# Nine k times v products per linear attention layer on GpSimd, and VectorE's own v operands only in PSUM

## The reference

```
# gated linear attention (first layer): the decay is k itself, its complement scales the key
kv[t] = decay[t] * kv[t-1] + key[t, d] * v[t, e]
h[t, e] = sum_d q[t, d] * kv[t, d, e]          ;  out = h @ out_w.T + out_b
# retention (second layer): decay is one constant per head, q scaled by 8**-0.5, then a group norm
# lightning attention (second layer): q, k, v = silu(x @ W), constant decay per head,
# then a layer norm of o and a gate: (o * sigmoid(x @ Wg1 @ Wg2)) @ Wo
```

## Time and profile before

| | |
|---|---|
| median of 3 runs | 1290.07 us (1289.89 to 1290.91) |
| the profiled execution | 1290.51 us, span 1288.8 us |
| gated loop, first scan to last z | 553.4 to 642.9 us |
| retention loop, first scan to last z | 687.0 to 774.6 us |
| lightning loop, first scan to last z | 987.3 to 1084.4 us |
| busy in the span | PE 77%, DVE 70%, ACT 39%, POOL 31% |

### The profile page before, as it was taken

How to read it: one execution, slowest core, us unless ns; L and a number is a source line. 1 busy time by engine, 2 the same in 40 slices (tenths; PEclk the granted TensorE clock), 3 DMA queues, 4 the chain that set the end, 5 groups by cost and what they waited for, 6 DMA issues and landing times. The chain is left out here.

```text
span 1288.8 us, 17437 instructions
## 1 busy us (share of the span) xinstructions
PE 989.6 (77%) x5856; PEld 498.2 (39%) x5856; DVE 903.9 (70%) x1529; ACT 507.7 (39%) x1042; POOL 400.1 (31%) x479
## 2 busy tenths in 40 slices
PE   5377898999999998686658665399966775459994
PEld 3222222222222323453543213266643444336663
DVE  6957889898888712889878995533347997643335
ACT  5234567787787685311021102033334221113333
POOL 3211111011101111444425441156633344226662
PEclk9557789899999999799679976599987985679997
DMA  6881000000000002312001211011121120101114
GB/s 127 180 188 16 2 1 1 1 2 2 2 1 2 2 2 92 118 60 65 25 1 43 72 33 33 13 38 43 43 74 59 41 63 4 33 19 42 44 42 115
DMA packets 52797, 56.18 MB, mean 44 GB/s; under 512 B 7956, under 2 KB 40092, under 8 KB 52700
## 3 DMA queue, kind: packets, MB, share of 16 engines
q1 hardware_dynamic: 47480, 44.78, 13.7%
q0 software_dynamic: 4992, 10.23, 3.0%
q10 hardware_dynamic: 240, 0.05, 0.0%
HBM read 37.94 MB, written 16.91 MB: 43 GB/s over the span
## 5 line engine op out<-in xcount | busy, mean ns | idle before, releaser
L720 DVE TENSOR_REDUCE mpart<-ps 128x2 f32<-128x1024 f32 (+3 forms) x320 | 325.2, 1060 | 63.2 <-PE ps L771 38.4
L841 ACT ACTIVATE arena<-ps 128x512 f32<-128x512 f32 (+3 forms) x640 | 292.2, 542 | 147.1 <-PE ps L788 137.8
L788 PE MATMUL ps<-arena 51*128 51x512 bf16 (+3 forms) x640 | 183.8, 375 | 14.1 <-ACT arena L841 5.7
L1071 POOL TENSOR_TENSOR arena<-arena 128x512 f32<-128x512 f32 x96 | 122.2, 1274 | 165.2 <-DVE arena L1124 165.2
L771 PE MATMUL ps<-arena 51*128 51x512 bf16 (+3 forms) x640 | 152.0, 388 | 23.5 <-DVE mpart L720 15.4
L802 PE MATMUL ps<-arena,w 128*32 128x512 f32 (+3 forms) x1280 | 161.2, 577 | 2.7 <-ACT arena L841 2.2
L690 POOL TENSOR_SCALAR_AFFINE_SELECT arena<-arena 128x512 f32<-128x512 f32 x64 | 40.6, 635 | 317.5 <-ACT arena L841 234.2
L1573 DVE COPY arena<-ps 128x128 f32<-128x128 f32 x78 | 22.7, 291 | 161.6 <-PE ps L1716 161.6
L1663 ACT ACTIVATE arena<-ps 128x512 f32<-128x512 f32 x78 | 46.6, 597 | 218.8 <-PE ps L1726 218.8
L788 PEld LDWEIGHTS ps<-arena 51*128 51x128 bf16 x640 | 50.4, 96 | 174.1 <-ACT arena L841 135.8
L1110 DVE TENSOR_TENSOR arena<-arena 128x512 f32<-128x512 f32 x62 | 102.1, 1646 | 12.4 <-ACT arena L1177 4.7
(11 more groups left out here) (263 smaller groups left out, 1490.9 us busy)
## 6 DMA issues: line engine op xcount, KB each, us to landing
w<-in_w SPq DMA_DIRECT2D x2, 2048.0 KB, 11.5
arena<-results SPq DMA_DIRECT2D x16, 256.0 KB, 4.9
arena<-g_v SPq DMA_DIRECT2D x15, 256.0 KB, 3.6
arena<-r_v SPq DMA_DIRECT2D x15, 256.0 KB, 3.6
arena<-l_v SPq DMA_DIRECT2D x15, 256.0 KB, 3.6
arena<-q_stack SPq DMA_DIRECT2D x8, 384.0 KB, 6.9
arena<-k_stack SPq DMA_DIRECT2D x8, 384.0 KB, 8.8
tokens<-arena SPq DMA_DIRECT2D x8, 256.0 KB, 2.4
```

What stands on the lines that cost most here:

```text
L720: nc.vector.tensor_reduce(out=mpart[:, 2 * pl:2 * pl + 2, t, kc], in_=ps[:, bank:bank + 2, 0:width], axis=AX.X, op=ALU.max).then_inc(ring_ ...
L788: nc.tensor.matmul(ps[:, n % ST, off:CH], rows(Ks, j % 2, 2 * g + j // 2, kt * P, (kt + 1) * P), rows(Qs, j % 2, 2 * g + j // 2, c * CH + ...
L841: nc.scalar.activation(probs[:, n % 2, j[0], off:CH], ps[:, (GH * n + j[0]) % ST, off:CH], ACT.Exp, scale=float(HD) ** -0.5).then_inc(exp_ ...
L1071: nc.gpsimd.tensor_tensor(z[:, n % ZB, :], state[:, n % SB, :], q[:, c % 2, :], ALU.mult).then_inc(z_ready, 1)
```

## The change

In all three layers:

- `by_dma` shrinks to e = 3, 5, 7 of the chunks 1 to 3, so nine products a layer. Their update is made by GpSimd (`by_pool`), which issues update(n + 3) right behind z(n).
- The other 23 products have v from TensorE, and VectorE makes their update with v read from PSUM. In the lightning layer ScalarE writes the silu back into the same PSUM bank, and the buffers `vs` are gone.
- `upd` has four buffers instead of two. VectorE's update(n) therefore waits for scan(n - 4) and no longer for scan(n - 2).
- In the lightning layer TensorE may write a bank of v again only when the update that reads it is done. Before it had to wait for ScalarE alone.
- A semaphore `upd_pooled` counts GpSimd's updates, and `wait_update` picks the semaphore for n.

```diff
-            by_dma = [n for n in range(NC * HD) if n >= HD and n % HD in (1, 3, 5, 6, 7)]
+            by_dma = [n for n in range(NC * HD) if n >= HD and n % HD in (3, 5, 7)]
             by_pe = [n for n in range(NC * HD) if n not in by_dma]
+
+            by_pool, by_dve = by_dma, by_pe
...
+            def wait_update(eng, n):
+                if n in by_pool:
+                    eng.wait_ge(upd_pooled, by_pool.index(n) + 1)
+                else:
+                    eng.wait_ge(upd_ready, by_dve.index(n) + 1)
...
                         nc.gpsimd.tensor_tensor(z[:, n % ZB, :], state[:, n % SB, :], q[:, c % 2, :], ALU.mult).then_inc(z_ready, 1)
+                        if n + 3 in by_pool:
+                            u = n + 3
+                            m = by_dma.index(u)
+                            pool.wait_ge(v_loaded[m % VB], 16 * (m // VB + 1))
+                            nc.gpsimd.tensor_tensor(upd[u % UB], vd[:, m % VB, :], k[:, u // HD % 2, :], ALU.mult).then_inc(upd_pooled, 1)
...
-                        if n in by_dma:
-                            m = by_dma.index(n)
-                            dve.wait_ge(v_loaded[m % VB], 16 * (m // VB + 1))
-                            v_in = vd[:, m % VB, :]
-                        elif kind == "lightning":
-                            m = by_pe.index(n)
-                            dve.wait_ge(v_out, m + 1)
-                            v_in = vs[:, m % 2, :]
-                        else:
-                            m = by_pe.index(n)
-                            dve.wait_ge(v_ready, m + 1)
-                            v_in = ps[:, 4 + m % 2, :]
+                        m = by_pe.index(n)
+                        dve.wait_ge(v_out if kind == "lightning" else v_ready, m + 1)
+                        v_in = ps[:, 4 + m % 2, :]
                         dve.wait_ge(kq_out, 2 * (n // HD) + 1)
-                        if n >= 2:
-                            dve.wait_ge(scanned, n - 1)
-                        nc.vector.tensor_tensor(upd[:, n % 2, :], v_in, k[:, n // HD % 2, :], ALU.mult).then_inc(upd_ready, 1)
+                        if n >= UB:
+                            dve.wait_ge(scanned, n - UB + 1)
+                        nc.vector.tensor_tensor(upd[n % UB], v_in, k[:, n // HD % 2, :], ALU.mult).then_inc(upd_ready, 1)
...
-                        if n + 1 < NC * HD:
+                        if n + 1 in by_dve:
                             update(n + 1)
-                        dve.wait_ge(upd_ready, n + 1)
+                        wait_update(dve, n)
...
-                            if m >= 2:
-                                act.wait_ge(upd_ready, by_pe[m - 2] + 1)
-                            nc.scalar.activation(vs[:, m % 2, :], ps[:, 4 + m % 2, :], ACT.Silu).then_inc(v_out, 1)
+                            nc.scalar.activation(ps[:, 4 + m % 2, :], ps[:, 4 + m % 2, :], ACT.Silu).then_inc(v_out, 1)
...
-                            if m >= 2 and kind == "lightning":
-                                pe.wait_ge(v_out, m - 1)
-                            if m >= 2 and kind != "lightning":
-                                pe.wait_ge(upd_ready, by_pe[m - 2] + 1)
+                            if m >= 2:
+                                wait_update(pe, by_pe[m - 2])
```

More of the change, by code:

```diff
@@ L1010, in linear_attention @@
             k = take(2 * CH).rearrange("p (b t) -> p b t", b=2)
-            dec = take(2 * CH).rearrange("p (b t) -> p b t", b=2)
-            vs = take(2 * CH).rearrange("p (b t) -> p b t", b=2)
-            upd = take(2 * CH).rearrange("p (b t) -> p b t", b=2)
+            spare = take(2 * CH)
+            dec = spare.rearrange("p (b t) -> p b t", b=2)
+            upd = take(2 * CH)
             SB, ZB = HD + 4, HD
@@ L1021, in linear_attention @@
             gate = take(T)
-            g1 = take(2 * CH)[0:HD, :].rearrange("p (b t) -> p b t", b=2)
+            low_rank = take(2 * CH)
+            g1 = low_rank[0:HD, :].rearrange("p (b t) -> p b t", b=2)
+            UB = 4
+            upd = [half[:, i * CH:(i + 1) * CH] for half in (upd, low_rank if kind == "gated" else spare) for i in (0, 1)]
             negb = take(1)
@@ L1041, in linear_attention @@
             upd_ready = sem(name + "_upd_ready")
+            upd_pooled = sem(name + "_upd_pooled")
             scanned = sem(name + "_scanned")
@@ L1124, in _ @@
                         nc.vector.tensor_tensor_scan(
-                            out=state[:, n % SB, :], data0=a, data1=upd[:, n % 2, :],
+                            out=state[:, n % SB, :], data0=a, data1=upd[n % UB],
                             initial=0.0 if c == 0 else state[:, (n - HD) % SB, CH - 1:CH],
@@ L1274, in _ @@
                             if m >= VB:
-                                sp.wait_ge(upd_ready, by_dma[m - VB] + 1)
+                                wait_update(sp, by_dma[m - VB])
                             sp.dma_start(vd[:, m % VB, :], bass.AP(tensor=v_dram.tensor, offset=c * P * CH + n % HD * CH,
```

## The result

The changed kernel takes 1269.34 us (median of 4 runs, 1268.12 to 1270.31) against 1290.45 before (1289.89 to 1290.91). The ratio is 0.9836, with a 95% interval of 0.9819 to 0.9853, and the saving is 21.1 us, 5 more than the 16 that were forecast. The profiled execution took 1268.4 us, its span 1266.7.

A forecast was written before the change was run, and what follows sets the result against it. It took a port shared by GpSimd and VectorE to bound the loops. Gains of 3.2 (gated), 2.3 (retention) and 10.2 (lightning), together 15.7, took 1290.5 to 1274.8, or 1274.4 us against the median; range 1266 to 1287.

The forecast's parts named there:

- The shared port bounds the loops, and an update with v in PSUM is free: All loops: GpSimd and VectorE instructions with two SBUF operands take turns; a product takes 2.43 us with v in PSUM, 3.08 in SBUF.
- A GpSimd instruction that waits costs 1.06 behind the scan: Loops: a GpSimd instruction already waiting ends 1.06 us behind the scan, so it and a waiting scan take 2.15, not 2.43.
- the first rival: All loops: the handover is not hidden, each product costs 2.43 us and each GpSimd update 1.26 on top; 1285.6 us, chance 0.20.
- Chunk 0 of lightning 4.8, of the others 0.65: From scan 0 to scan 8: gain of 4.8 us in lightning, 0.65 each in gated and retention, where only update 9 changes.
- The walk of chunks 1 to 3, 64.2: Both queues from scan 8 to the end of z 31: 64.2 us; gains 4.0 gated, 2.1 retention, 7.4 lightning before deductions.
- the lower edge of its range: All layers: 8 x 0.26 x 3 = 6 us less if scans behind GpSimd's updates lose nothing; own range 1266 to 1280.
- The additions of the gated layer: Bias additions between scans 13 and 14 of each chunk: up to 0.55 us of the port, three times; taken at 1.0.
- TensorE late at e = 6: k and q made ahead of v of e = 6 wait for z: deducted 2.0 us in lightning, 0.5 in each other layer.
- the layers without silu pay less: Gated and retention, having no silu, lose less to TensorE's lateness: 0.5 us each against 2.0 in lightning.
- Four buffers gain nothing by themselves: Update buffers: four remove a wait of VectorE that lay under z, with no gain by itself.
- TensorE as the bound: Lightning, chunks 1 to 3: TensorE limits; 1282.8 us if its clock stays as before (chance 0.07), near 1311 at 1.2 GHz (0.08).
- the clock is higher where TensorE is busier: Lightning: argument against TensorE limiting; granted clock 1.00, 0.93, 0.79, 0.64 at 89, 72, 76 and 61% busy.

The follow-up runs named there:

- e1: Changed kernel with no product on GpSimd or from DRAM: all 32 updates a layer on VectorE with v from PSUM; 1255.29 us.
- e7: All 32 updates a layer on VectorE from PSUM, none on GpSimd, as a variant of the changed kernel, but with two update buffers instead of four; 1258.41 us.
- e8: Changed kernel with all updates on VectorE, written back over v in PSUM, where the scan reads them; three banks for v; 1217.43 us.
- e4: Changed kernel with TensorE issuing k and q of the next chunk ahead of the add_product of e = 1; 1265.84 us.
- e5: Kernel before with only one part of the change, four buffers for the updates instead of two; 1278.29 us.
- e3: Changed kernel with the nine products a layer updated by VectorE with v from SBUF, GpSimd making z only; 1263.65 us.
- e6: Changed kernel with twelve updates a layer on GpSimd instead of nine (e = 1, 3, 5, 7), v from DRAM; 1277.57 us.

## Why the prediction was right, step by step

- *The shared port bounds the loops, and an update with v in PSUM is free.* Shown: by e1 (2.43 us a product, expected and measured), e7, and e8, where taking the second SBUF operand from the scan ends the exclusion.
- *A GpSimd instruction that waits costs 1.06 behind the scan.* Right: pairs of 2.15 all through the changed kernel, so the first rival (1285.6) is out. This was the step said to be the likeliest to fail.
- *Chunk 0 of lightning 4.8, of the others 0.65.* Right: A fell by 4.8, 0.7 and 0.7.
- *The walk of chunks 1 to 3, 64.2.* Its prices held, its order not: behind GpSimd's update z goes first, not the scan. This term was 2.6 us too dear in retention (61.6 in e4) and in lightning (61.6). The order makes 2.1 of it, which the prediction had named as the lower edge of its range (8 x 0.26 a layer). Most of the 5 us that the forecast lacks come from here: B gained 2.6, 3.4 and 9.2, where 2.5, 1.6 and 5.4 were forecast with the deductions inside. In the gated layer the agreement of 2.6 and 2.5 is luck: the additions (1.4 dearer than taken) and TensorE (1.1 dearer) took back what the walk had too much.
- *TensorE late at e = 6.* Right in kind and place, but its size was right by luck. The waits were longer (2.3 and 3.4 us in the gated layer): TensorE had stood idle for 3.12 us ahead of the second one, and its granted clock was 0.50 in the work that followed. The price is 3.8 us by e4's loops, where 3.0 were taken, but it fell elsewhere than forecast: 1.6 in the gated layer, 1.4 in retention and 0.8 in lightning, where 0.5, 0.5 and 2.0 were taken. That the layers without silu pay less is wrong.
- *The additions of the gated layer.* Taken at 1.0; without TensorE's lateness the gated B is 2.4 above retention's (64.0 and 61.6 in e4), so it was too small. In e1, where GpSimd has no z left over to fill the gap, the difference is 3.9 (61.0 and 57.1). The prediction priced the port alone (0.55 each) and put VectorE's own time in the additions at nothing, without a reason. No run takes the additions alone.
- *Four buffers gain nothing by themselves.* Wrong as a statement: e5 gains 13.6 us by them alone. In this change it made no error in the sum, since no update of VectorE with v in SBUF is left, and e7 shows no gain from them then. That is luck: the prediction did not give this as its reason.
- *TensorE as the bound.* Out: its clock was higher, as was forecast. The argument for it, that the clock is higher where TensorE is busier, is not shown: in the third chunk of lightning it was busy 76% of the time in both kernels, at a granted clock of 0.79 before and 1.00 now. The prices of the rival were too high as well (e1, e8).
- *What the sum did not ask* is whether GpSimd's nine updates were worth making. They are not: they cost 5.7 us against leaving them on VectorE from SBUF (e3), and 14 us against v from PSUM everywhere (e1). The change is fast by its other parts (e3).

## What to carry to other kernels

Where a VectorE instruction's duration depends on where its operand lies (1.76 and 0.69 us here), look at what GpSimd does at that moment, and count the time that both need in turn, not the busy time of each. Where the two take turns, as here, moving work from VectorE to GpSimd lengthens the path that it seems to relieve (0.57 us for each update in e6). Moving one operand to PSUM shortens it, and the longest instruction (here the scan, 1.27 us instead of 1.92) is the one to free first.

## What the runs showed that was not expected

- The start decides who waits. Released from a wait for the scan ahead, the same update started 0.16 us ahead of z instead of 0.05 behind it, took 0.66 instead of 1.76 us, and a product 2.78 instead of 3.08 (e3, e5).
- An instruction that already waits needs less time behind the one that it waits for than it takes alone: z ends 1.06 us behind the scan where z alone takes 1.26, and the scan 1.09 behind z where it alone takes 1.27. On the first the difference between 1274 and 1286 in the prediction hung. The Trainium skill (SBUF — State Buffer, "SBUF: two separate sides") says that of a VectorE instruction with two SBUF inputs and a GpSimd instruction that reads SBUF, whichever starts first gets the shared port pair for the whole instruction and the other fully blocks. The rows agree that they take turns (2.15 us a pair). The section does not say how much of its own time an instruction that waited still needs. The prediction read it as speaking against 1.06, and it does not. That the 0.2 us are start-up done while waiting is an inference; no run shows what they are.
- The exclusion ends with the second SBUF operand. A scan with the decay and its output in SBUF and its data in PSUM ran beside z at 1.27 us, and z at 1.28 (e8).
- ScalarE and VectorE can write a result over its own operand in a PSUM bank at no extra cost: silu 0.58 us in place (e8) against 0.60 into SBUF (before), update 0.68 in place (e8) against 0.67 into SBUF (changed kernel).
